# The order of VectorE's instructions and the gates on GpSimd's gathers in a software pipeline of graph attention

## The chip, the cores and the metric

The kernel runs on one core of a Trainium2 chip. The metric is the device time of one execution in microseconds (us).

## The reference

A graph of 6250 nodes with 64 features and 206,250 edges, sorted by their destination. One layer of mean aggregation is followed by three layers of attention (heads: 2, 2, 1; 64 channels in all). Cut to what matters, with H heads of C channels:

```python
def _transformer_conv(x, src, dst, eattr, ...):
    q, k, v = x @ Wq + bq, x @ Wk + bk, x @ Wv + bv     # each reshaped to (n, H, C)
    e = (eattr @ We).reshape(-1, H, C)
    kj = k[src] + e
    alpha = jnp.sum(q[dst] * kj, axis=-1) / jnp.sqrt(jnp.float32(C))
    m = jax.ops.segment_max(alpha, dst, num_segments=n)
    a = jnp.exp(alpha - m[dst])
    s = jax.ops.segment_sum(a, dst, num_segments=n)
    a = a / (s[dst] + 1e-16)
    vj = v[src] + e
    out = jax.ops.segment_sum(a[..., None] * vj, dst, num_segments=n)
    return out.reshape(n, H * C) + x @ Ws + bs
```

## The kernel before

The edges are cut into blocks of 1024, 8 columns (T) of 128 edges. Each pass over the edges has 202 steps, one for each block: one pass for the mean layer, three for attention. Between the passes are node phases that work out the tables of k, v and q for the nodes.

An attention pass is a software pipeline of five stages, Z, A, B, C, D, each a step later than the one before it. In step t the engines work on stage Z of block t+2, A of t+1, B of t, C of t-1 and D of t-2. What each engine does in a step, and in which order, is written out by hand: `vector_step` (L990), `tensor_step` (L1070), `scalar_step` (L1133), and the lists `order` (L666) from which the semaphore values are worked out. Every instruction of such a list raises its engine's progress semaphore by one, and `after(e, engine, op, s)` waits until an instruction of block s is done. `hold(e)` is an increment of a spare semaphore behind such a wait.

VectorE's 24 instructions of a step, by the names used below:
- Stage A: `kj` (L752) and `vj` (L757) add the edge term to the gathered rows of k and v; `prod` (L763) multiplies by q, `alpha` (L768) sums over the channels; `flag` (L774) and `scan` (L782) make the running maximum over edges with one destination; `O` (L720) is the one-hot matrix of edge and destination.
- Stage Z: `OT` (L731) is the transposed one-hot, from int16 to bf16, 1024 elements in each partition; `cont` (L743) and `last` (L737) mark the borders of segments.
- Stage B: `fhi`, `fm` (L785), `flo`, `cr`, `X`, `Mhi`, `Mm`, `Mlo`, `df` spread the maxima over the edges.
- Stage C: `d1`, `d`, and `vals` (L837), which multiplies vj by the weights.
- Stage D: `facc` (L863) and `acc` (L873) rescale and add up the result in `acc`.

GpSimd does one thing in an attention pass: for each block eight indirect DMAs, one for each column j (L1355, `gathers`), each of which fetches 128 rows of the table KV by the indices in `sdn` into the buffer `G`. There are three buffers G, so gathers may run ahead of VectorE. The first blocks are unrolled, where only gather 0 waits, for `vj` of three blocks ago. In the loop the table `gates` says which gather waits for what: gather 0 of block s for `aT` (a TensorE transpose, in the step after which `alpha` is known) of block s-3. `kj` of block s waits until all eight gathers of block s have landed.

TensorE's aggregation `agg` of block dt writes pG, which `facc` and `acc` read; before it stands a wait for `acc` of block dt-1. SyncE loads the indices, edge features and q rows of a block, behind a wait for `O` of three blocks ago (L1247).

Of the kernel before, what the change touches and what calls it, by code (L numbers as in the profile page):

```python
# [66 lines left out]
def build(nc, z, a, ctx):  # L67
    B, NCOL, NT, SM = z.blocks, z.nc, z.tiles, z.smax
# [15 lines left out]
    acc = sb("acc", [66, NCOL])  # L84
# [570 lines left out]
    def edge_pass(name, kind, l, heads, qtab, kvtab, eat):  # L655
# [8 lines left out]
        AR = 64 + H  # L664
        if att:
            order = {  # L666
                "V": ["A kj", "A vj", "B fhi", "B fm", "B flo", "B cr", "Z OT", "A prod", "A alpha", "C d1", "C d",
                      "Z cont", "Z last", "A flag", "A O", "B X", "B Mhi", "B Mm", "B Mlo", "B df", "C vals",
                      "D facc", "D acc", "A scan"],
                "P": ["B Fb", "A q", "D agg7", "B Mn", "Z e", "A aT", "B Me"],  # L670
                "A": ["A tb", "A lb", "A Ob", "C w", "B fb", "B fbw"],
            }
        else:
            order = {
                "V": ["C acc", "Z O", "Z OT"],
                "P": ["A e", "B agg7", "A q"],
                "A": ["A relu"],
            }
# [20 lines left out]
        def after(e, k, o, s):  # L699
            e.wait_ge(prog[k], val(k, o, s))  # L700
# [24 lines left out]
        def v_OT(e, s):  # L725
            u = s.slot
            if att:
                ge16(e, s_l, NL, s)
            else:
                ge16(e, s_d, 1, s)  # L730
            return e.tensor_scalar(OTs[u][:, :, :].rearrange("p j m -> p (j m)"), db[u][:, :],  # L731
                                   bfp[:, bass.ds(s.value(), 1)], None, ALU.is_equal)
# [257 lines left out]
        def vector_step(e, t, on):  # L990
            pV = prog["V"]
            zt, at, bt, ct, dt = t + 2, t + 1, t, t - 1, t - 2
            if not att:
                if "C" in on:
                    v_acc(e, ct).then_inc(pV, 1)
                else:
                    missing(e, "V", t, "acc", "acc")
                if "Z" in on:
                    v_O(e, zt).then_inc(pV, 1)
                    v_OT(e, zt).then_inc(pV, 1)  # L1000
                else:
                    missing(e, "V", t, "O", "OT")
                return
            if "A" in on:
                v_kj(e, at).then_inc(pV, 1)
                v_vj(e, at).then_inc(pV, 1)
            else:
                missing(e, "V", t, "kj", "vj")
            if "B" in on:
                v_fhi(e, bt).then_inc(pV, 1)  # L1010
                v_fm(e, bt).then_inc(pV, 1)
                v_flo(e, bt).then_inc(pV, 1)
                v_cr(e, bt).then_inc(pV, 1)
            else:
                missing(e, "V", t, "fhi", "cr")
            if "Z" in on:
                v_OT(e, zt).then_inc(pV, 1)
            else:
                missing(e, "V", t, "OT", "OT")
            if "A" in on:  # L1020
                v_prod(e, at).then_inc(pV, 1)
                v_alpha(e, at).then_inc(pV, 1)
            else:
                missing(e, "V", t, "prod", "alpha")
            if "C" in on:
                if "B" not in on:
                    after(e, "P", "Me", ct)
                v_d1(e, ct).then_inc(pV, 1)
                v_d(e, ct).then_inc(pV, 1)
            else:  # L1030
                missing(e, "V", t, "d1", "d")
            if "Z" in on:
                v_cont(e, zt).then_inc(pV, 1)
                v_last(e, zt).then_inc(pV, 1)
            else:
                missing(e, "V", t, "cont", "last")
            if "A" in on:
                v_flag(e, at).then_inc(pV, 1)
                v_O(e, at).then_inc(pV, 1)
            else:  # L1040
                missing(e, "V", t, "flag", "O")
            if "B" in on:
                v_X(e, bt).then_inc(pV, 1)
                v_Mhi(e, bt).then_inc(pV, 1)
                v_Mm(e, bt).then_inc(pV, 1)
                v_Mlo(e, bt).then_inc(pV, 1)
                if "A" not in on:
                    after(e, "A", "fbw", bt - 1)
                v_df(e, bt).then_inc(pV, 1)
            else:  # L1050
                missing(e, "V", t, "X", "df")
            if "C" in on:
                v_vals(e, ct).then_inc(pV, 1)
            else:
                missing(e, "V", t, "vals", "vals")
            if "D" in on:
                if "A" not in on:
                    after(e, "P", "agg7", dt)
                if "C" not in on:
                    after(e, "V", "acc", dt - 1)  # L1060
                v_facc(e, dt).then_inc(pV, 1)
                v_acc(e, dt).then_inc(pV, 1)
            else:
                missing(e, "V", t, "facc", "acc")
            if "A" in on:
                v_scan(e, at).then_inc(pV, 1)
            else:
                missing(e, "V", t, "scan", "scan")

        def tensor_step(e, t, on):  # L1070
            pP = prog["P"]
            zt, at, bt, dt = t + 2, t + 1, t, t - 2
            if not att:
                if "A" in on:
                    p_e0(e, at).then_inc(pP, 1)
                else:
                    missing(e, "P", t, "e", "e")
                if "B" in on:
                    for j in range(T - 1):
                        p_agg(e, bt, j)  # L1080
                    p_agg(e, bt, T - 1).then_inc(pP, 1)
                else:
                    missing(e, "P", t, "agg7", "agg7")
                if "A" in on:
                    for j in range(T - 1):
                        p_q(e, at, j)
                    p_q(e, at, T - 1).then_inc(pP, 1)
                else:
                    missing(e, "P", t, "q", "q")
                return  # L1090
            if "B" in on:
                p_Fb(e, bt).then_inc(pP, 1)
            else:
                missing(e, "P", t, "Fb", "Fb")
            if "A" in on:
                for j in range(T - 1):
                    p_q(e, at, j)
                p_q(e, at, T - 1).then_inc(pP, 1)
            else:
                missing(e, "P", t, "q", "q")  # L1100
            if "D" in on:
                after(e, "V", "acc", dt - 1)
                hold(e)
                p_fac(e, dt)
                for j in range(T - 1):
                    p_agg(e, dt, j)
                p_agg(e, dt, T - 1).then_inc(pP, 1)
            else:
                missing(e, "P", t, "agg7", "agg7")
            if "B" in on:  # L1110
                p_Mc(e, bt)
                for j in range(T):
                    p_Mn(e, bt, j)
                p_Mn(e, bt, T).then_inc(pP, 1)
            else:
                missing(e, "P", t, "Mn", "Mn")
            if "Z" in on:
                p_e0(e, zt)
                p_e1(e, zt).then_inc(pP, 1)
            else:  # L1120
                missing(e, "P", t, "e", "e")
            if "A" in on:
                p_aT(e, at).then_inc(pP, 1)
            else:
                missing(e, "P", t, "aT", "aT")
            if "B" in on:
                for j in range(T - 1):
                    p_Me(e, bt, j)
                p_Me(e, bt, T - 1).then_inc(pP, 1)
            else:  # L1130
                missing(e, "P", t, "Me", "Me")
# [203 lines left out]
                for c in range(3 + z.peel, 6 + z.peel):  # L1335
                    pool_step(e, At(i, c))

        gates = {0: ("P", "aT", 3)}

        AHEAD = 2  # L1340

        def gathers(e, s):
            u = s.slot
            ge16(e, s_i, 1, s)
            hold(e)
            for j in range(T):
                if isinstance(s.i, int):
                    if j == 0 and not fresh(s):
                        after(e, "V", "vj", s - 3)
                        hold(e)  # L1350
                elif j in gates:
                    engine, op, behind = gates[j]
                    after(e, engine, op, s - behind)
                    hold(e)
                e.indirect_dma_start(G[u][:, j, :], None, kvtab,  # L1355
                                     bass.IndirectOffsetOnAxis(ap=sdn[u][:, j:j + 1], axis=0)).then_inc(s_g[u], 16)
# [155 lines left out]
```

## Time and profile before

| what | value |
|---|---|
| runs, median (lowest to highest) | 6918.2 us (6917.99 to 6919.75), 3 runs |
| the profiled execution | 6918.2 us, its span 6916.5 us |
| TensorE busy | 4425.5 us (64%) |
| VectorE busy | 4457.8 us (64%) |
| ScalarE busy | 969.0 us (14%) |
| GpSimd busy | 4794.7 us (69%) |
| mean DMA rate | 98 GB/s |

Busy time counts only the execution of instructions, not the time an engine takes between two of them or waits. The three attention passes are alike and much the longest part.

### The profile page before, as it was taken

Reading aid. Unit: us, or ns where it says so; the run is one execution under the profiler, and the core shown is the slowest. Engines: PE = TensorE matmul, PEld = TensorE weight load, DVE = VectorE, ACT = ScalarE, POOL = GpSimd, SP = SyncE. Lnnn points to the kernel's source line nnn. Section 1 sums busy time; section 2 is a strip of 40 time slices with the busy share of each in tenths; the row PEclk is TensorE's granted clock in tenths of the full one; section 3 lists DMA queues with packets and bytes.
Section 4 is the critical chain, followed back from the end, with each engine's and each line's share of the span. In section 5 each row is a group of like instructions: output and inputs, shape, how many; then the busy total and the mean of one; then the engine's idle time right before and its main releaser. Section 6 shows DMA issues by size and latency. Waiting matters only on the chain. (4 is left out here: it accounts for less than half of the span.)

```text
span 6916.5 us, 148957 instructions
## 1 busy us (share of the span) xinstructions
PE 4425.5 (64%) x36620; PEld 3474.0 (50%) x36620; DVE 4457.8 (64%) x15728; ACT 969.0 (14%) x4122; POOL 4794.7 (69%) x5118
## 2 busy tenths in 40 slices
PE   6996666666666666666666666666656666666665
PEld 5775444444444446444444444446444444444444
DVE  6556666666666666666666666666666666666666
ACT  2222111111111112111111111112111111111110
POOL 2224777777777774777777777775777777777775
PEclk8996555555555555555555555555555555555555
DMA  4553333333333333333333333333333333333333
GB/s 120 159 159 96 94 94 95 94 96 95 94 94 93 95 94 90 95 94 96 95 95 95 93 94 94 94 93 88 99 93 96 94 94 95 94 97 95 94 94 75
DMA packets 687686, 675.83 MB, mean 98 GB/s; under 512 B 369234, under 2 KB 506388, under 8 KB 687636
## 3 DMA queue, kind: packets, MB, share of 16 engines
q0 software_dynamic: 161600, 320.52, 19.4%
q1 hardware_dynamic: 496944, 301.76, 16.5%
q10 hardware_dynamic: 29092, 52.97, 2.6%
q8 instruction: 20, 0.33, 0.0%
q14 instruction: 30, 0.25, 0.0%
HBM read 652.96 MB, written 21.67 MB: 98 GB/s over the span
## 5 line engine op out<-in xcount | busy, mean ns | idle before, releaser
L1355 POOL DMA_INDIRECT Gall<-KV,sdn x4848 | 4647.3, 959 | 1516.8 <-issue 1337.4
L752 DVE TENSOR_TENSOR kj<-Gall,pE 128x512 f32<-128x512 f32 x606 | 416.7, 688 | 1896.3 <-DMA Gall<-KV,sdn 1894.2
L946 PE MATMUL pG<-O,vals 128*66 128x42 f32 (+1 forms) x10784 | 1297.9, 308 | 0.7 <-ACTq L988 0.7
L946 PEld LDWEIGHTS pG<-O,vals 128*66 128x66 f32 (+1 forms) x10784 | 1207.1, 223 | 46.9 <-ACT vals L982 26.1
L932 PE MATMUL pY<-fw,Ob 128*42 128x6 bf16 (+1 forms) x4848 | 257.9, 176 | 1056.8 <-DVE cr L805 1043.7
L959 ACT ACTIVATE fw<-lm 128x16 bf16<-128x16 f32 (+1 forms) x606 | 135.9, 224 | 5348.4 <-DVE O L720 5348.4
L932 PEld LDWEIGHTS pY<-fw,Ob 128*42 128x42 bf16 x4848 | 223.0, 121 | 1111.3 <-issue 1111.0
L879 PE MATMUL pE<-bd,ea 128*128 128x256 f32 x1212 | 739.9, 714 | 13.5 <-PEq L988 13.5
L939 PEld LDWEIGHTS pM<-Mb,OTs 42*128 42x128 bf16 x4848 | 178.1, 101 | 952.7 <-issue 952.7
L884 PE MATMUL pE<-bd,ea 128*128 128x256 f32 x1212 | 642.7, 634 | 0.0
L916 PE MATMUL pS<-ident,Fs 16*128 16x16 f32 (+1 forms) x606 | 152.2, 251 | 733.3 <-DVE Fs L782 729.5
L939 PE MATMUL pM<-Mb,OTs 42*128 42x6 bf16 (+1 forms) x4848 | 212.3, 163 | 545.5 <-DVE df L823 543.4
L916 PEld LDWEIGHTS pS<-ident,Fs 16*128 16x128 f32 (+1 forms) x606 | 107.6, 177 | 768.1 <-issue 768.1
L837 DVE TENSOR_TENSOR vals<-vj,vals 128x512 f32<-128x512 f32 x606 | 420.0, 693 | 69.4 <-ACT vals L977 6.8
L884 PEld LDWEIGHTS pE<-bd,ea 128*128 128x128 f32 x1212 | 407.9, 337 | 108.5
L720 DVE SCALAR_TENSOR_TENSOR O<-sdn,bf,iof 128x336 f32<-128x336 int32 x808 | 451.6, 559 | 5.6 <-DVEq L988 1.3
L731 DVE TENSOR_SCALAR OTs<-db,bfp 128x1024 bf16<-128x1024 int16 x808 | 418.1, 517 | 21.3 <-DMA dr<-in_dr 18.2
L768 DVE TENSOR_REDUCE al<-kj 128x16 f32<-128x512 f32 (+1 forms) x606 | 416.4, 687 | 20.9
L757 DVE TENSOR_TENSOR vj<-Gall,pE 128x512 f32<-128x512 f32 x606 | 412.0, 680 | 0.0
L763 DVE TENSOR_TENSOR kj<-kj,pQ 128x512 f32<-128x512 f32 x606 | 409.5, 676 | 1.3 <-PEq L988 0.7
L1252 POOL DMA_DIRECT2D sdn<-in_sdn x202 | 108.8, 539 | 400.1 <-DVE OTs L731 333.8
L904 PE MATMUL pQ<-qw,OTs 128*128 128x64 bf16 x4848 | 367.7, 241 | 8.6 <-DVEq L988 6.1
(185 smaller groups left out, 6275.8 us busy)
## 6 DMA issues: line engine op xcount, KB each, us to landing
db<-D SPq DMA_DIRECT2D x606, 256.0 KB
ea<-in_ea SPq DMA_DIRECT2D x606, 128.0 KB
Gall<-KV,sdn POOLq DMA_INDIRECT x4848
db<-D ACTq DMA_DIRECT2D x202, 256.0 KB, 3.7
qw<-QT SPq DMA_DIRECT2D x1818, 5.2 KB
dr<-in_dr SPq DMA_DIRECT2D x1212, 4.0 KB
ea<-in_ea SPq DMA_DIRECT2D x202, 64.0 KB, 3.7
sdn<-in_sdn SPq DMA_DIRECT2D x606, 12.0 KB
```

Source lines behind the costliest of these rows:

```text
L720: return e.scalar_tensor_tensor(O[u][:, :, :], sdn[u][:, T:2 * T].unsqueeze(2).to_broadcast([128, T, W]), bf[:, bass.ds(s.value(), 1)], io ...
L731: return e.tensor_scalar(OTs[u][:, :, :].rearrange("p j m -> p (j m)"), db[u][:, :], bfp[:, bass.ds(s.value(), 1)], None, ALU.is_equal)
L752: return e.tensor_tensor(kj[:, :, :], G[u][:, :, 0:64], pE[u][:, :].rearrange("p (j c) -> p j c", c=64), ALU.add)
L757: return e.tensor_tensor(vj[u][:, :, :], G[u][:, :, 64:128], pE[u][:, :].rearrange("p (j c) -> p j c", c=64), ALU.add)
L763: return e.tensor_tensor(kj[:, :, :], kj[:, :, :], pQ[:, :].rearrange("p (j c) -> p j c", c=64), ALU.mult)
L768: return e.tensor_reduce(al[u][:, 0:H * T].rearrange("p (h j) -> p j h", h=H), kj[:, :, :].rearrange("p j (h c) -> p j h c", h=H), AX.X, A ...
L837: return e.tensor_tensor(vals[u][:, :, 0:64].rearrange("p j (h c) -> p j h c", h=H), vj[u][:, :, :].rearrange("p j (h c) -> p j h c", h=H) ...
L879: return e.matmul(pE[u][:, 0:256], ea[u][:, 0:128], bd32[:, l, :], start=True, stop=True)
L884: return e.matmul(pE[u][:, 256:512], ea[u][:, 128:256], bd32[:, l, :], start=True, stop=True)
L932: return e.matmul(pmn[:, j, :], lhs, rhs, start=False, stop=j == T)
L946: return e.matmul(sums[u][0:AR, 0:W], vals[u][:, j, 0:AR], O[u][:, j, :], start=j == 0, stop=j == T - 1)
L1355: e.indirect_dma_start(G[u][:, j, :], None, kvtab, bass.IndirectOffsetOnAxis(ap=sdn[u][:, j:j + 1], axis=0)).then_inc(s_g[u], 16)
```

## The change

`OT` moves in VectorE's order from behind `cr` to behind `df`; `facc` and `acc` move from behind `vals` to behind `O`; `scan` now stands ahead of `vals`, which comes last. The wait in front of `agg` asks for `vals` of the same block instead of `acc` of the block before. The table of gates gives six of the eight gathers a wait on VectorE, gather 0 for `Mlo` of block s-3 instead of TensorE's `aT`, and the gathers 1, 2, 5, 6 and 7, which had none, for `scan`, `vals`, `vj`, `prod` and `flag`. All values of the semaphore follow from the lists. The mean pass is not touched.

```diff
             order = {
-                "V": ["A kj", "A vj", "B fhi", "B fm", "B flo", "B cr", "Z OT", "A prod", "A alpha", "C d1", "C d",
-                      "Z cont", "Z last", "A flag", "A O", "B X", "B Mhi", "B Mm", "B Mlo", "B df", "C vals",
-                      "D facc", "D acc", "A scan"],
+                "V": ["A kj", "A vj", "B fhi", "B fm", "B flo", "B cr", "A prod", "A alpha", "C d1", "C d", "Z cont",
+                      "Z last", "A flag", "A O", "D facc", "D acc", "B X", "B Mhi", "B Mm", "B Mlo", "B df", "Z OT",
+                      "A scan", "C vals"],
...
             if "D" in on:
-                after(e, "V", "acc", dt - 1)
+                after(e, "V", "vals", dt)
                 hold(e)
                 p_fac(e, dt)
...
-        gates = {0: ("P", "aT", 3)}
+        gates = {0: ("Mlo", 3), 1: ("scan", 2), 2: ("vals", 4), 5: ("vj", 1), 6: ("prod", 1), 7: ("flag", 1)}
...
                 elif j in gates:
-                    engine, op, behind = gates[j]
-                    after(e, engine, op, s - behind)
+                    op, behind = gates[j]
+                    after(e, "V", op, s - behind)
                     hold(e)
```

In `vector_step` the calls of v_OT, v_facc with v_acc, and v_scan move in the same way.

## Rows read from the trace of the kernel before

**Rows 1.** Stretches of the first and the last attention pass: GpSimd's gathers, clock, DMA share.

```profile
601.00:2651.00 2050.00, 1555.96 (x1616) 0.50 0.38 95
...
4827.00:6867.00 2040.00, 1542.71 (x1616) 0.50 0.38 95
sum 6137.00, POOL 4647.31; mean POOL 1549.10
```

**Rows 2.** Groups by line; then the gathers' durations (min/median/max) and landing.

```profile
L1355 POOL DMA_INDIRECT Gall<-KV,sdn x4848 | 4647.3, 959 | 1516.8 <-issue 1337.4
L752 DVE TENSOR_TENSOR kj<-Gall,pE 128x512 f32<-128x512 f32 x606 | 416.7, 688 | 1896.3 <-DMA Gall<-KV,sdn 1894.2
...
L1355 POOL DMA_INDIRECT Gall<-KV,sdn x4848: 940/944/1537, 601.0 to 6865.0; - x194
...
DMA to landing us min/median/max: 2.5/3.9/5.4
```

**Rows 3.** Waits of SyncE's DMA queue: us in total, times, longest.

```profile
SPq L708 <- DVE O L720: 2969.6, 596, 6.5
```

**Rows 4.** Order in time, VectorE, one step: start us, us, instruction.

```profile
2002.30 0.69 DVE L752 TENSOR_TENSOR kj<-Gall,pE 128x512 f32<-128x512 f32 x1 [3.08 <-DMA Gall<-KV,sdn]
...
2004.01 0.59 DVE L731 TENSOR_SCALAR OTs<-db,bfp 128x1024 bf16<-128x1024 int16 x1
...
2006.35 0.28 DVE L774 TENSOR_TENSOR flg<-tb 16x127 f32<-16x127 f32 x1
2006.56 0.55 DVE L720 SCALAR_TENSOR_TENSOR O<-sdn,bf,iof 128x336 f32<-128x336 int32 x1
...
2007.62 0.15 DVE L823 TENSOR_TENSOR df<-X,Mm 42x2 f32<-42x2 f32 x1
...
2007.87 0.69 DVE L837 TENSOR_TENSOR vals<-vj,vals 128x512 f32<-128x512 f32 x1
...
2008.58 0.21 DVE L863 TENSOR_SCALAR acc<-acc,pG  x1
...
2008.94 0.40 DVE L782 TENSOR_TENSOR_SCAN Fs<-flg,pS 16x128 f32<-16x128 f32 x1
...
2012.21 0.69 DVE L752 TENSOR_TENSOR kj<-Gall,pE 128x512 f32<-128x512 f32 x1 [2.87 <-DMA Gall<-KV,sdn]
```

**Rows 5.** GpSimd in the same step: gathers 5 and 7 and the next gather 0.

```profile
2005.90 0.94 POOL L1355 DMA_INDIRECT Gall<-KV,sdn  x1 [0.31 <-issue]
...
2008.39 0.99 POOL L1355 DMA_INDIRECT Gall<-KV,sdn  x1 [0.30 <-issue]
2009.69 0.94 POOL L1355 DMA_INDIRECT Gall<-KV,sdn  x1 [0.30 <-issue]
```

**Rows 6.** Three long gathers and what VectorE had under way.

```profile
882.02 0.48 DVE L731 TENSOR_SCALAR OTs<-db,bfp 128x1024 bf16<-128x1024 int16 x1
882.42 0.68 DVE L763 TENSOR_TENSOR kj<-kj,pQ 128x512 f32<-128x512 f32 x1
...
882.19 1.13 POOL L1355 DMA_INDIRECT Gall<-KV,sdn  x1 [0.30 <-issue]
...
1027.48 0.27 DVE L774 TENSOR_TENSOR flg<-tb 16x127 f32<-16x127 f32 x1
1027.68 0.55 DVE L720 SCALAR_TENSOR_TENSOR O<-sdn,bf,iof 128x336 f32<-128x336 int32 x1
...
1027.62 1.43 POOL L1355 DMA_INDIRECT Gall<-KV,sdn  x1 [0.30 <-issue]
...
2088.71 0.69 DVE L837 TENSOR_TENSOR vals<-vj,vals 128x512 f32<-128x512 f32 x1
...
2089.08 1.14 POOL L1355 DMA_INDIRECT Gall<-KV,sdn  x1 [0.30 <-issue]
```

**Rows 7.** The first and the last of the 4848 gathers.

```profile
601.05 1.01 POOL L1355 DMA_INDIRECT Gall<-KV,sdn  x1 [12.70 <-DMA KV<-stg]
...
6865.05 0.94 POOL L1355 DMA_INDIRECT Gall<-KV,sdn  x1 [0.30 <-issue]
```

More of the change, by code:

```diff
@@ L1015, in vector_step @@
                 missing(e, "V", t, "fhi", "cr")
[L1016 to L1019, printed above, removed]
             if "A" in on:
@@ L1041, in vector_step @@
                 missing(e, "V", t, "flag", "O")
+            if "D" in on:
+                if "A" not in on:
+                    after(e, "P", "agg7", dt)
+                if "C" not in on:
+                    after(e, "V", "acc", dt - 1)
+                v_facc(e, dt).then_inc(pV, 1)
+                v_acc(e, dt).then_inc(pV, 1)
+            else:
+                missing(e, "V", t, "facc", "acc")
             if "B" in on:
@@ L1051, in vector_step @@
                 missing(e, "V", t, "X", "df")
+            if "Z" in on:
+                v_OT(e, zt).then_inc(pV, 1)
+            else:
+                missing(e, "V", t, "OT", "OT")
+            if "A" in on:
+                v_scan(e, at).then_inc(pV, 1)
+            else:
+                missing(e, "V", t, "scan", "scan")
             if "C" in on:
@@ L1055, in vector_step @@
                 missing(e, "V", t, "vals", "vals")
[L1056 to L1059, printed above, removed]
-                    after(e, "V", "acc", dt - 1)
[L1061 to L1068, printed above, removed]
         def tensor_step(e, t, on):
@@ L1101, in tensor_step @@
             if "D" in on:
-                after(e, "V", "acc", dt - 1)
+                after(e, "V", "vals", dt)
                 hold(e)
```

## The prediction

> **What bounds the kernel now.** I read the stretches first, then the groups by line, the waits, and then the order in time of one step. The page's list of engines is no help by itself: no engine is over 70% busy. The stretches show that the three attention passes fill most of the span [rows 1]: 2050 us the first, 2040 the last, 6137 in sum for 606 steps, or 10.1 us a step; each holds 1616 gathers that keep GpSimd busy some 1550 us. The rest, 6916.5 - 6137 = 780 us of setup, mean pass and node phases, is left as it is by the change.
>
> The groups show why a share of 69% hides the bound [rows 2]. The 4848 gathers are busy for 4647.3 us, 959 ns each, and stand behind 1516.8 us of idle time, 1337.4 of it put down to "issue": GpSimd waits for nobody, it needs 0.30 us between two gathers. A gather is 940 ns at the least and 944 at the median, and up to 1537. So the pace of a step is 8 x (0.944 + 0.300) = 9.95 us of bare gathers, plus (959 - 942) ns x 4848 = about 80 us over the kernel by which some gathers are longer. VectorE instead waits 1894.2 us in front of `kj` for the gathered rows, 3.1 us a step. Anything that shortens or rearranges VectorE's work changes nothing directly; only what lengthens a gather or the gap between gathers moves the time.
>
> **What lengthens a gather.** The order in time answers this [rows 6]. The gather at 1027.62 took 1.43 us; `O` began at 1027.68 while `flag` was under way since 1027.48, and ended at 1028.23. Take the time from 0.12 us after the gather's start to `O`'s end: 1028.23 - 0.12 - 1027.62 = 0.49, and the gather lost 1.43 - 0.94 = 0.49. The gather at 2089.08 took 1.14, with `vals` from 2088.71 to 2089.40: 2089.40 - 0.12 - 2089.08 = 0.20, and that is what it lost. The gather at 882.19 took 1.13, with `OT` from 882.02 to 882.50: 0.19 by the same sum, 0.19 lost. So a gather that is 0.12 us old while `flag`, `O`, `vals` or `OT`, begun before it, still runs, is held until that ends. One that was there first loses nothing: at 2005.90 it takes 0.94 although `O` starts at 2006.56 [rows 4, 5]. By that rule I put the long gathers of the whole trace (counted over all 4848, the first and the last are in [rows 7]) to their causes: `vals` 35 us, `flag` with `O` 26, `OT` 7, `fhi` and `fm` 7, the small rest is spread out. That makes up the 80.
>
> The Trainium skill (SBUF — State Buffer, Who interferes with whom) says that a VectorE instruction with two SBUF inputs contends with a GpSimd one that reads SBUF, one in a two-port mode with any, and that whoever issues first holds the shared ports. The trace agrees with the order of issue. The same section infers that `tensor_tensor` does not stall descriptor generation; by that only `OT` could cost anything here, but `vals` is a tensor_tensor and the 1.14 us gather under it says otherwise.
>
> **The change, part by part.**
> 1. *Five more gates* (gathers 1, 2, 5, 6, 7; gather 0 changes its own). Do they block? kj of the step of rows 4 starts at 2002.30. Gather 7 starts at 2008.39, 6.1 us after it, gather 0 of the next block at 2009.69, 7.4 us after, and the data of gather 7 let the next kj go at 2012.21 [rows 4, 5]. Each gate asks for an instruction of the VectorE step that is under way: gather 7 for `flag`, which ended 4.3 us after kj and will end at about 3.9; gather 0 for `Mlo`, which ends at about 5.2; `scan` and `vals` end at about 6.1 and 6.8, and gathers 1 and 2 come at 8.6 and 9.9. So each has 2 to 3 us in hand. The landing (2.5 to 5.4 us, median 3.9) seldom is late by more than that. Blocking: 0 to 5 us, I take 0.
>  Do they cost by being there? Gather 0 in the loop has two waits and two marker increments in front of it, others have none, and the idle time before it is 0.30 like that before the rest: the row at 2009.69 is a gather 0 [rows 5]. The work in between lies under the 0.94 us of the gather before. Cost 0. If that cover were not there, the nearest row for a price is the gap itself: half of it again, 0.15 us for each of five, would be 0.75 x 606 = 450 us; this bound I hold to be far off.
> 2. *OT leaves the place after cr*. In [rows 6] `prod` starts 0.40 after `OT`, and as a rule 0.42. So `prod`, `alpha`, `flag` and `O` all come 0.42 us sooner after kj: `flag` to 3.6, `O` to 3.8, ending at 4.35 (now 4.0, 4.2, 4.8 as a rule; this step was 0.06 late).
>  Gather 5 starts 3.6 us after kj here (2005.90), and over the 606 steps between 3.4 and 4.1 in eight of ten. Today it is mostly there before `O`. From the new place it is held when it starts between 3.67 (flag is under way) and 4.35 - 0.12 = 4.22. Of 601 gathers that start 3.2 to 4.45 us after a kj, 388 lie in that stretch and are short of its end by 119 us in sum; with only those after `O`'s own start it is 225 and 47 us. The same two counts for the old place give 37 and 5.5 us, and the long gathers there came to 26, which is two thirds of the way up. The same two thirds of 47 to 119 is 93 us. Net +67 us, bounds +21 and +93.
> 3. *facc and acc go before X*. `facc` starts at 2008.58 and `scan` at 2008.94, so the pair takes 0.36 us. Neither causes long gathers. `vals` used to wait for ScalarE: df starts at 2007.62, lasts 0.15, and vals starts at 2007.87. The read of the accumulator's address, which lay under a `vals` of 0.69, now has an `O` of 0.55 as cover; 0 to 0.15 us later from there on. GpSimd doesn't see that but by phase.
> 4. *OT after df, scan, then vals last*. df will start at 3.8 + 0.48 + 0.36 + 0.58 = 5.2, `OT` at 5.3 to 5.8, `scan` at 5.7, `vals` at 6.05 to 6.75. Gather 7 stands at 5.84 to 6.61 in eight of ten. Held by the new vals are starts between 6.13 and 6.63: 355 of 600, 99 us in sum, against 35 now. (For the old place the count gives 34 us, so it can be trusted.) But part 2 has shifted those behind a held gather 5: they go on at 4.22 + 1.24 = 5.46, where the new `OT` is under way and can hold gather 6 by 5.8 - 0.12 - 5.46 = 0.22 us, or miss it by a hair; a gather 7 after both comes at 6.7 to 6.95, past the end of vals' stretch. The two exclude each other for much of the steps. I take 60 us for vals and 30 for OT, less the 35 and 7 of now: +48 us. Bounds: 0 to +120.
> 5. *What else moves.* `agg` now waits for `vals` instead of `acc` of the step before: that ends at 6.8 and PE has until `acc`, 4 us after the next kj. `scan` ends earlier than before, so the transposes behind it are early. SyncE's loads wait for `O` (2969.6 us in all, [rows 3]), which comes 0.42 us sooner: no loss. VectorE's step has the same instructions, about 7 us, and still waits 3 us for the gather. All 0.
>
> The profiled execution was 6918.2 us, as the median, for a span of 6916.5. Sum: 6918 + 67 + 48 = 7033; I give 7030. About 0.2%, 14 us, is what a measurement here can tell from no change.
>
> **Rivals.**
> - *The new places miss the gathers.* What counts is where `flag`, `O`, `OT` and `vals` start relative to gathers 5, 6 and 7. If the new VectorE order has the step 0.3 us tighter or looser than my timetable, or the phases lock in a kinder way after the first hold, the long gathers vanish. Were all gone: 6918 - 80 = 6838; more likely half, 6880. It decides when the four instructions hold no more than today: with vals and OT at their lower bound, when fewer than about 110 gathers 5 are held (26 us at 93 / 388 = 0.24 each). Against it: the count over real starts in part 2 does not depend on anything after `O`. 0.17.
> - *Nothing measurable.* The gains and losses cancel, or `flag` and `O` hold a gather less than they did: 6918. By the skill's inference above, as a mechanism here, only OT is left, 7 us now and 10 to 40 later: 6920 to 6950; the row of the 1.14 us gather speaks against it. 0.13 in all within 0.2%.
> - *The gates cost in the gap.* Five waits and increments not hidden; at 0.05 us each 0.25 x 606 = 150 us on top of the sum: 7180, or alone 7070. The equal gap of gather 0 is against it. 0.07.
> - *The gates bind.* Then GpSimd would be led by VectorE: needs landings over 6 us, and the longest is 5.4. 0.01.
>
> **How the numbers follow.** Longer gathers as summed: 0.62, own range 6960 to 7100 (terms at +21 and +20, to +93 and +90). Slower altogether 0.62 + 0.07 + 0.01 = 0.70, same 0.13, faster 0.17. The range from 6900 to 7110 leaves out most of the faster case and of the gap's cost.
>
> **What would show it.** VectorE's order in time: OT after df, `O` ending 4.3 us after kj. The gather's mean up from 959 to 983 ns (115 us over 4848), the longest ones at position 5 under `O`, then 7 under `vals`, or 6 under `OT`. Idle before the gathers unchanged at about 1517 us with 0.30 each; any more is the gates'. kj's wait goes up by 0.2 us a step. Wrong if the mean is at or under 959, or if the gaps before gated gathers are over 0.30.

## The result and the profile after

The changed kernel takes 7155.15 us (median of 4, 7152.58 to 7170.39) against 6918.26 us: ratio 1.0344, 95% interval 1.0327 to 1.0361. It is slower by 237 us, as forecast in sign, and more than twice as much as forecast (+112), outside the range. Its profiled execution took 7176.55 us, 258.35 more than that of before (6918.2).

The groups hold the answer to [rows 2]. First two groups by line of the changed kernel (busy us, mean ns, idle before), then, from the view of the tile, the durations of the gathers (min/median/max in ns):

```profile
L1355 POOL DMA_INDIRECT Gall<-KV,sdn x4848 | 4905.9, 1012 | 1515.8 <-issue 950.6
L752 DVE TENSOR_TENSOR kj<-Gall,pE 128x512 f32<-128x512 f32 x606 | 417.0, 688 | 2225.1 <-DMA Gall<-KV,sdn 2222.5
```

```profile
L1355 POOL DMA_INDIRECT Gall<-KV,sdn x4848: 940/944/1767, 600.9 to 7122.8; - x194
```

The gathers are busy for 4905.9 - 4647.3 = 258.6 us more, and that is the whole difference of the two profiled executions. The idle time before them is 1515.8 against 1516.8: six gates instead of one cost nothing here. The median gather is 944 ns as before, so a part of them has become much longer.

One step in order of time shows which. It answers to [rows 4, 5] (start us, us, instruction). First VectorE; then GpSimd with gather 7 of one block, gathers 5, 6 and 7 of the next:

```profile
2005.13 0.69 DVE L752 TENSOR_TENSOR kj<-Gall,pE 128x512 f32<-128x512 f32 x1 [4.16 <-DMA Gall<-KV,sdn]
...
2008.92 0.55 DVE L720 SCALAR_TENSOR_TENSOR O<-sdn,bf,iof 128x336 f32<-128x336 int32 x1
...
2010.48 0.62 DVE L731 TENSOR_SCALAR OTs<-db,bfp 128x1024 bf16<-128x1024 int16 x1
2011.03 0.40 DVE L782 TENSOR_TENSOR_SCAN Fs<-flg,pS 16x128 f32<-16x128 f32 x1
2011.35 0.66 DVE L837 TENSOR_TENSOR vals<-vj,vals 128x512 f32<-128x512 f32 x1
```

```profile
2002.42 0.94 POOL L1355 DMA_INDIRECT Gall<-KV,sdn  x1 [0.30 <-issue]
...
2009.91 0.94 POOL L1355 DMA_INDIRECT Gall<-KV,sdn  x1 [0.30 <-DVE acc L873]
2011.16 1.67 POOL L1355 DMA_INDIRECT Gall<-KV,sdn  x1 [0.30 <-DVE OTs L731]
2013.13 0.94 POOL L1355 DMA_INDIRECT Gall<-KV,sdn  x1 [0.30 <-issue]
```

VectorE stands within 0.2 us of where the prediction put it (medians: flag 3.6, O 3.8, OT 5.35, scan 5.9, vals 6.2 us after kj; forecast for the last three 5.3, 5.7, 6.05). Two things were not foreseen.

First, gather 6 at 2011.16 took 1.67 us. By the rule of the prediction it should have been safe: 0.12 us after its start, at 2011.28, `scan` was running, under which no gather had been held before, and `vals` began only at 2011.35. Yet it was held to the end of vals: 2012.01 - 0.12 - 2011.16 = 0.73, and it lost 1.67 - 0.94 = 0.73. Over all steps, 343 gathers begin under scan and 328 are held; the 15 others began within 0.05 us of scan's start. In the kernel before it was 72 and none; but there the instruction behind scan is the next `kj`, which still waits for its data.

Second, the gathers stand elsewhere. Gather 7 here is that at 2002.42; its data let kj go at 2005.13, 1.77 us after its end. This time from the end of gather 7 to the start of kj is called the landing from here on. In [rows 4, 5] it was 2012.21 - 2009.38 = 2.83. The medians over 606 steps are 1.76 and 2.73. Since GpSimd goes on at its own pace and kj comes sooner after gather 7, all gathers stand later after kj: gathers 5, 6, 7 at 4.8, 6.05 and 7.9 us instead of 3.9, 5.1 and 6.4. So gather 5 goes free behind `O`, and gather 6 begins just under `scan`.

Sorted by the instruction at whose end the held gather goes on, the long gathers sum to 339 us (80 before): vals 281 (33), O 22 (20), OT 14 (6), flag 3 (3); the rest, 18 (19), ends with none of the four. These sums, here and below, are the busy time of all 4848 gathers of a trace less 0.942 us for each.

### The profile page after: what moved, and what is told of

Same layout as the page of the kernel before. It is cut to its first block and busy times, and to the rows that moved or that the text cites. A ratio compares the mean times of both kernels' runs of the same rounds, so it can differ in the third digit from the quotient of the medians.

```text
span 7174.9 us, 154717 instructions
## 1 busy us (share of the span) xinstructions
PE 4422.2 (62%) x36620; PEld 3475.0 (48%) x36620; DVE 4453.4 (62%) x15728; ACT 997.8 (14%) x4122; POOL 5053.5 (70%) x5118
## 5 line engine op out<-in xcount | busy, mean ns | idle before, releaser
L1355 POOL DMA_INDIRECT Gall<-KV,sdn x4848 | 4905.9, 1012 | 1515.8 <-issue 950.6
L884 PEld LDWEIGHTS pE<-bd,ea 128*128 128x128 f32 x1212 | 407.5, 336 | 109.2
L837 DVE TENSOR_TENSOR vals<-vj,vals 128x512 f32<-128x512 f32 x606 | 396.8, 655 | 3.0 <-DVEq L988 1.8
L879 PEld LDWEIGHTS pE<-bd,ea 128*128 128x128 f32 x1212 | 303.5, 311 | 24.7 <-issue 14.6
```

What stands on the lines that cost most here:

```text
L837: return e.tensor_tensor(vals[u][:, :, 0:64].rearrange("p j (h c) -> p j h c", h=H), vj[u][:, :, :].rearrange("p j (h c) -> p j h c", h=H) ...
L879: return e.matmul(pE[u][:, 0:256], ea[u][:, 0:128], bd32[:, l, :], start=True, stop=True)
L884: return e.matmul(pE[u][:, 256:512], ea[u][:, 128:256], bd32[:, l, :], start=True, stop=True)
L1355: e.indirect_dma_start(G[u][:, j, :], None, kvtab, bass.IndirectOffsetOnAxis(ap=sdn[u][:, j:j + 1], axis=0)).then_inc(s_g[u], 16)
```

## The experiments

The runs were made on several chips, each with the kernel before beside it; ratios are to that. The kernel before itself took 6918 us (median) with the result above, 6970 beside the first four experiments, 6939 beside the next four and 6960 beside the test of the loads. On three more chips, called slow below, it took some 8700 us; they are told of last. Each chip had one set of runs, so chip and time can't be told apart. So a ratio near 1 says little here without the trace. Its profiled execution at 6918.2 us is the yardstick for the rows: in every trace of the fast chips the time is that plus what the gathers' busy and idle time are above 4647.3 + 1516.8, within 4 us.

**Gates alone.**

```diff
-        gates = {0: ("P", "aT", 3)}
+        gates = {0: ("Mlo", 3), 1: ("scan", 2), 2: ("vals", 4), 5: ("vj", 1), 6: ("prod", 1), 7: ("flag", 1)}
...
```

> The old order of VectorE with the six new gates. If the gates are free (the gaps of the changed kernel sum to 1515.8 us as before): 6918 us within 15, mean of a gather 959 ns, idle before gathers 1517 us. If the gates are part of the loss, because they tie the gathers to VectorE: at least 60 us slower and the idle before gathers grows.

7031.98 us, ratio 1.0084 (1.0061 to 1.0107): 62 us above the kernel before on this chip, with more idle time, so the second expectation by its numbers. Group of the gathers, and a gather 1:

```profile
L1355 POOL DMA_INDIRECT Gall<-KV,sdn x4848 | 4714.3, 972 | 1561.6 <-issue 1064.3 <-DVE cr L805 78.0 <-DVE flg L774 54.0
```

```profile
3431.56 0.94 POOL L1355 DMA_INDIRECT Gall<-KV,sdn  x1 [1.62 <-issue]
```

The idle time grew by 45 us, made of 45 gaps of 0.66 to 2.02 us in front of gather 1, one every 13 steps of a pass, with no wait for anybody. Some of the same steps show such a gap in other kernels: 2 in the changed kernel, 32 of 0.5 to 1.5 us in the changed kernel with three waits (below), none in the order alone, and 45 of some 2.0 us in a kernel with the one old gate on a slow chip (below). Why they come is open. The larger part of what the trace has above that of the kernel before is the long gathers, 147 us instead of 80 (vals 60, O 38, OT 23), for the gathers stand elsewhere: gather 6 at 5.8 and gather 7 at 7.25 us after kj, with a landing of 2.36. So VectorE is not waited for in the old order either, which was the mechanism of that expectation, but the gates were not free there.

**Order alone.** The changed kernel with the old table of gates.

> The new order of VectorE with the one old gate. If the order alone makes the loss through longer gathers: 7155 us within 20, mean of a gather 1012 ns, most of it at gather 6. If order and gates only cost together: under 7050.

7174.23 us, ratio 1.0291 (1.0271 to 1.0310), long gathers 339 us, gather 6 held in 495 of 606 steps. The ratio is smaller than that of the changed kernel because the kernel before took 6970 us on this chip.

```profile
L1355 POOL DMA_INDIRECT Gall<-KV,sdn x4848 | 4905.8, 1012 | 1513.5 <-issue 1469.4 <-DMA KV<-stg 28.4 <-DVE fm L785 4.5
```

Busy time and mean are those of the changed kernel (4905.9, 1012): the order alone makes the loss, and with this order the gates have no part in it.

**vals waits for scan.** The changed kernel with one more wait.

```diff
             after(e, "A", "w", s)
+            after(e, "V", "scan", s + 2)
             return e.tensor_tensor(
```

> The changed kernel with one more wait: vals starts only when scan is done. Theory A: an instruction that needs the shared ports holds them from when it is queued behind a running one, so that vals behind scan holds for 1.05 us instead of 0.65; with the wait it can't queue, and a gather that begins under scan is not held. The sum by which gathers are longer falls from 337 us to under 220, time under 7050. Theory B: scan itself or any work in that place holds the gather: time stays at 7155 within 20, gathers are still held when they begin under scan. The wait itself costs VectorE under 0.1 us a step, of the 3.7 us that it idles.

6910.66 us, ratio 0.9912 (0.9894 to 0.9929). One wait took away the whole loss: 264 us against the order alone on the same chip. Long gathers 74 us, 6 less than in the trace of the kernel before. That the ratio is 0.9% under 1 isn't explained by that; it compares with 6970 us on this chip, where the kernel before was not profiled.

```profile
L1356 POOL DMA_INDIRECT Gall<-KV,sdn x4848 | 4640.4, 957 | 1514.8 <-issue 776.8
```

The same situation as above, in order of time:

```profile
5468.19 0.40 DVE L782 TENSOR_TENSOR_SCAN Fs<-flg,pS 8x128 f32<-8x128 f32 x1
5468.62 0.69 DVE L838 TENSOR_TENSOR vals<-vj,vals 128x512 f32<-128x512 f32 x1
```

```profile
5468.31 0.95 POOL L1356 DMA_INDIRECT Gall<-KV,sdn  x1 [0.31 <-issue]
```

The gather begins under scan and takes 0.95; 279 begin so, none is held, though vals starts within 0.5 us behind them, as in the changed kernel. scan itself holds nobody, theory B falls. What holds is vals when it stands behind a running scan with nothing left to wait for. In the kernel before it stood behind df, and there is idle time in front of it, as far as the trace names it for ScalarE. The groups of vals, before and changed:

```profile
L837 DVE TENSOR_TENSOR vals<-vj,vals 128x512 f32<-128x512 f32 x606 | 420.0, 693 | 69.4 <-ACT vals L977 6.8
L837 DVE TENSOR_TENSOR vals<-vj,vals 128x512 f32<-128x512 f32 x606 | 396.8, 655 | 3.0 <-DVEq L988 1.8
```

Theory A, that it takes the ports while still queued, explains it; the trace shows only that the wait ends it. The wait also changed the places (landing 2.04, gathers 5, 6, 7 at 4.5, 5.8, 7.1), so not all of the 259 us is the queueing itself.

**O waits for flag,** in the kernel before.

```diff
                 after(e, "P", "agg7", s - 3)
+                after(e, "V", "flag", s)
```

> The kernel before with one more wait: O starts only when flag is done. Theory A: gathers are no longer held through O from a start under flag; the 26 us by which flag and O lengthen gathers fall by 5 to 15, time 6900 to 6915. Theory B: no change from the wait but a later O: 6918 within 8 or slower by some us as O comes nearer to the next gather.

6911.91 us, ratio 0.9911 (0.9896 to 0.9927). O holds for 12.5 us in sum against 20, and wherever it holds a gather it had begun at least 0.16 us before the gather did (in the kernel before it held gathers that began up to 0.16 us ahead of it, while it was queued behind flag). That is as theory A has it. The kernel gains nothing by it: the long gathers sum to 82 us (80 in the kernel before), as vals has 37 instead of 33, and the profiled execution took 6918.07 us, as that of the kernel before did. The time is in the forecast range, but the ratio is again one to the 6970 us of this chip.

**The kernel before again.**

> The kernel before, unchanged, for its trace on the same chip as the runs beside it. Where it ran at 6970 us the gathers should be longer by the 52 us against 6918 (some 130 us in sum over 0.942 each instead of 80), not the gaps. If the gaps grew, the theory that only long gathers move this kernel is wrong.

6934.43 us, ratio 0.9993 (0.9983 to 1.0003), the same. This was not the chip of the four runs above, so the 130 us expected at 6970 stay untested. On this one the profiled execution took 6926.69 us, 8.5 more than the yardstick, with long gathers of 90 us (9 more) and an idle time of 1517.7 (1 more): the difference between these two traces is in the long gathers, not the gaps.

**Three waits,** vals for scan, O for flag, OT for df, on the changed kernel, and the like (OT for cr, O for flag, vals for df) on the kernel before.

> The changed kernel with waits that keep OT, O and vals from being queued behind df, flag and scan. Theory A (held from the queue): also the 9 us of O and some of OT's 26 go; 6880 to 6905 us, sum of long gathers 50 to 70 us. Theory B (only vals behind scan matters): as with that wait alone, 6911 within 8.

> The kernel before with waits that keep OT, O and vals from being queued behind cr, flag and df. vals already waited for ScalarE, so by theory A its wait does nothing; OT behind cr of 0.2 us: a few us. 6900 to 6912 us, about that of the kernel before with the wait of O alone. If more than 15 us below that one, the queue holds in more places than the runs have shown.

Ratios 1.0075 (1.0062 to 1.0088) and 1.0171 (1.0157 to 1.0184): both expectations missed, and with them the idea that more waits are better. In the changed kernel the long gathers sum to 137 us, 80 of them by vals, which holds gather 7. The kernel before with three waits, one step (VectorE, then gather 7):

```profile
4003.08 0.69 DVE L754 TENSOR_TENSOR kj<-Gall,pE 128x512 f32<-128x512 f32 x1 [3.15 <-DMA Gall<-KV,sdn]
...
4009.03 0.69 DVE L840 TENSOR_TENSOR vals<-vj,vals 128x512 f32<-128x512 f32 x1 [0.20 <-ACT vals L980]
```

```profile
4009.30 1.24 POOL L1358 DMA_INDIRECT Gall<-KV,sdn  x1 [0.30 <-issue]
```

The waits put OT 0.25, O 0.43 and vals 0.52 us later after kj. vals now begins at 6.05, gather 7 at 6.35, and it is held in some 540 of 606 steps (in the rows: 4009.72 - 0.12 - 4009.30 = 0.30, lost 0.30); O holds gather 6 in some 350. Long gathers 221 us: vals 149, O 48, OT 9. Each of flag, O, OT and vals, where it holds a gather, had begun at least 0.1 us before it: queueing is gone, the place alone does this.

**vals last,** in the kernel before: facc, acc and scan ahead of vals, OT, flag and O as they were. As in the change, `agg` then waits for `vals` of its block.

```diff
-  ... "B df", "C vals", "D facc", "D acc", "A scan"],
+  ... "B df", "D facc", "D acc", "A scan", "C vals"],
...
-                after(e, "V", "acc", dt - 1)
+                after(e, "V", "vals", dt)
```

> The kernel before with one part of the change: facc, acc and scan go ahead of vals, so that vals stands behind scan, ready to go; OT, flag and O stay. Theory A: vals holds from under scan, gathers that begin there are held for up to 1.05 - 0.12 us and the time rises by 50 to 250 us. Theory B (the loss is OT's or O's new place): within 20 us of the kernel before.

7037.11 us, ratio 1.0145 (1.0128 to 1.0162); long gathers 192 us, vals 95 of them, O 56, OT 25. 85 gathers begin under scan and 69 are held. vals behind scan is enough for a loss; for the large one more gathers must stand there.

**Where the landing comes from.** Over the traces of the fast chips it falls as gather 7 stands later than `O`, behind which SyncE's loads of a block wait (medians, us). Gates alone falls out of the line by some 0.3:

| kernel | gather 7 after O's start | landing after its end |
|---|---|---|
| before, three waits | 1.7 | 2.79 |
| before | 2.2 | 2.73 |
| before, vals last | 2.5 | 2.40 |
| changed, three waits | 3.0 | 2.09 |
| before, gates alone | 3.1 | 2.36 |
| changed, vals waits for scan | 3.3 | 2.04 |
| changed | 4.1 | 1.76 |

The largest load of a block is that of `db`, 256 KB. SyncE issues it here at these times, in the kernel before (the step of rows 4) and in the changed one:

```profile
2008.41 0.33 SPq L1266 DMA_DIRECT2D db<-D  x1
...
2010.76 0.33 SPq L1266 DMA_DIRECT2D db<-D  x1
```

Gather 7 ended at 2009.38 in the kernel before, 1.0 us after that, and in the changed one at 2013.13 + 0.94 = 2014.07, 3.3 us after. Sorted by this time and not by kernel, the steps of ten traces of the fast chips (all but the test below) fall together, gates alone too; a kernel with over 50 steps in a class lies within 0.25 us of the value given:

| end of gather 7 after the start of the large load, us | 1.0 | 1.5 | 2.0 | 2.5 | 3.0 | 3.5 |
|---|---|---|---|---|---|---|
| landing, median us | 2.8 | 2.6 | 2.25 | 2.0 | 1.7 | 1.7 |
| steps | 1672 | 849 | 1394 | 988 | 597 | 370 |

The test moves the loads and not the order, in the changed kernel:

```diff
-                after(e, "V", "O", s - 3)
+                after(e, "V", "scan", s - 3)
```

> The changed kernel with SyncE's loads of a block waiting for scan instead of O, 1.9 us later. Theory L (the loads stand in the way of a gather's data): gather 7, 7.9 us after kj, is again near the loads, its data take 2.3 to 2.8 us instead of 1.76, all gathers start 0.6 to 1.0 us sooner after kj, gather 6 leaves its place under scan and vals and O holds gather 5 more often, as the prediction had it; the time changes by more than 30 us, either way. Rival (the landing has to do with where gather 7 stands, not with the loads): landing 1.8 within 0.2, gather 6 at 6.05, 7155 to 7175 us. On a chip with late loads, where the kernel before takes 8700 us, the run says nothing of this.

7101.37 us, ratio 1.0205 (1.0188 to 1.0222). The landing is 2.53 in the median (1.76 without), and mostly up to 3.6; gathers 5, 6, 7 start 4.0, 5.5, 6.9 us after kj, 0.6 to 1.1 sooner. Long gathers 244 us: O 59, OT 49, vals 119. With the loads behind O, gather 7 at 7.0 and 7.1 us after kj had a landing of 2.09 and 2.04 (three waits, vals waits for scan), so the rival, that its place sets the landing, falls: the loads do slow the gathers' data. Within this trace, the 182 steps whose gather 7 ended some 0.5 us after the start of the large load have a landing of 3.37, the 149 where that load began 1 us after the end have 1.72. The change had taken the loads out of the way of gather 7: `O` came 0.4 us sooner, and the shorter landing and the held gathers then put gather 7 itself 1.5 us later after kj. Of 138 gathers that begin under scan, 124 are held.

**The chips on which the kernel before takes 8700 us.** The expectations speak of one chip with late loads; it was three, and no trace shows that the loads are what makes them slow. Four kernels, two with SyncE's loads moved (waiting for X of block s-4 in the changed kernel, for scan of block s-3 in the kernel before) and two with OT behind X, vals waiting for scan, and six gates or one. They ran twice, and one of them a third time, on a third such chip; the kernel before took 8690 to 8720 us beside them.

> The changed kernel; SyncE's loads of a block wait for X instead of O, so they start some 0.5 us later in the step, as late after kj as before the change. Theory L: a gather's landing is slowed by these loads; the change brought them forward, so the last gather's data came 1.76 us after its end instead of 2.73, which moved all gathers from 3.9, 5.1, 6.4 us after kj to 4.8, 6.05, 7.9, with gather 6 just under scan and vals. With the loads later the landing goes back to 2.3 us or more, gather 6 is off that place and the time falls under 7100. Rival: the landing is shorter because gather 7 itself stands later; then it stays at 1.8 within 0.2 and the time at 7155 to 7175.

> The kernel before; SyncE's loads wait for scan instead of O, some 2.2 us later in the step. Theory L: the landing of the last gather (median 2.6 to 2.7 us after its end) changes by more than 0.4 us, because the loads fall otherwise on it, and with it the places of the gathers and the sum of long gathers (80 to 90 us before). Rival: the landing does not depend on the loads, and landing and time stay (within 0.1 us and 15 us).

> The changed kernel with the wait of vals for scan (6911 us before), and OT moved on from behind df to behind X, 0.5 us earlier, to 4.8 to 5.3 us after kj, between gathers 5 and 6. If place alone decides, OT's 26 us of long gathers go and the sum falls from 78 to 45 to 60 us: 6880 to 6900 us, 0.985 to 0.990 of the kernel before. If OT behind another instruction holds as vals did behind scan, no gain or a loss.

> The same with the one old gate. If the gates only wait for what is long done: the same time within 10 us. If the five more cost (the old order with new gates showed 47 us more idle time before gathers): faster by up to 40 us.

> The changed kernel with SyncE's loads waiting for X instead of O, again, where the kernel before runs at 6918 to 6970 us. Theory L (the loads slow the landing of a gather): landing of the last gather back from 1.76 to 2.3 us or more after its end, gather 6 no longer at 6.05 us after kj, time under 7100. Rival (the landing is set by where gather 7 stands): 1.8 within 0.2, time 7155 to 7175.

> The kernel before with SyncE's loads waiting for scan instead of O, 2.2 us later. Theory L: landing differs from 2.6 to 2.7 us by more than 0.4, gathers shift against kj by as much, and the sum of long gathers leaves 80 to 90 us. Rival: landing within 0.1, time within 15 us.

> The changed kernel with vals waiting for scan and OT behind X, 4.8 to 5.3 us after kj. Place alone: sum of long gathers 45 to 60 us, 0.985 to 0.990 of the kernel before. If OT behind another instruction holds as vals behind scan did: no gain over 0.991.

> The same with the one old gate. If gates cost nothing where they do not block: within 10 us of the one with six gates. If five more cost: faster by up to 40 us.

> The changed kernel with vals waiting for scan and OT behind X, at 4.8 to 5.3 us after kj, between the places of gathers 5 (4.5) and 6 (5.8) that the wait alone showed. By place alone OT's 26 us of long gathers go, the sum falls from 78 to 45 to 60 us, and the ratio to the kernel before from 0.991 to 0.985 to 0.990. If the gathers' places shift with it (they hang on the landing, which moved by up to 1 us between the kernels), the sum can come out anywhere from 50 to 150 and the ratio up to 1.005. On a chip with late loads it says nothing.

Ratios: changed with later loads 1.0014 and 1.0010; before with later loads 1.1143 and 1.1135; OT behind X 1.0269, 1.0265 and 1.0291; with the old gate 1.0502 and 1.0508. None of them can answer what was asked, since another thing sets the pace. The waits of the first (us in total, times, longest):

```profile
DVE X L809 <- remote: 1793.7, 459, 7.5
...
POOL Gall L1355 <- DVE OTs L731: 791.3, 264, 14.4
...
DVE kj L752 <- DMA Gall<-KV,sdn: 377.0, 124, 6.6
```

VectorE hardly waits for gathers there (377 us against 2222 in the changed kernel above), but for something that the trace calls remote, that is, no instruction in it. And where VectorE is late GpSimd waits for it too: 791 us behind OT. In the kernel with OT behind X the gates wait 1794 us for scan:

```profile
POOL Gall L1359 <- DVE Fs L782: 1794.2, 527, 16.7
```

In the kernel before with later loads GpSimd waits 2580.6 us for the load of the indices, `sdn`. The kernel before itself was not profiled on these chips. Here six gates are faster than one (1.027 against 1.050), the opposite of a cost. Why these chips are slow, and whether OT behind X would win on the others, stays open.

## Why the prediction was wrong

- *GpSimd sets the pace, and only longer gathers or gaps move the time:* right, to 0.3 us (258.6 for 258.35).
- *Gates (part 1):* right for the changed kernel: no blocking, idle 1516 us. Order alone gives the same busy time. The argument, that the work of a gate is hidden, doesn't hold in general: with the old order the same gates came with 45 us of gaps.
- *OT leaves the place after cr (part 2):* the times of flag and O were right to 0.05 us. The term was +67; measured +3 (O and flag, 25 us against 22), because gather 5 was no longer there. With the loads moved back, and the landing near what the prediction took for fixed, it came to 59, two thirds of the 93.
- *scan ahead of vals (part 4) is the step that failed.* It sized vals at 60 us and OT at 30; they measured 281 and 14. Two assumptions in it were false. That a gather is held only by an instruction that has begun: vals, ready behind scan, holds from under it. The prediction had noted this for O behind flag and did not carry it over to vals, which by being put last no longer had anything to wait for. And that the places of the gathers after kj stay as they were but for the holds: they hang on the landing, and the landing on `O`, for SyncE's loads wait for it. The step of part 5 was the hole: "SyncE's loads wait for `O` [...], which comes 0.42 us sooner: no loss."
- *The sum:* the forecast had the sign, with +115 us of long gathers for the +259 measured. Its parts were off both ways, by 64 us too much in part 2 and by 208 too little in part 4 (vals and OT +256 for +48), so the sum is nearer than its larger part by luck. Its own range took part 4 at +20 to +90, whose bounds it had given as 0 to +120; the wider ones would not have reached either.
- How much is whose: with the wait for scan the whole loss goes (74 us of long gathers), with the loads moved back 244 of 339 us remain. That speaks for the queueing as the larger cause; their shares can't be parted, as each hold moves the places again.
- *The rival "The new places miss the gathers"* came true for O alone; the other three did not happen in the changed kernel.
- The Trainium skill (SBUF — State Buffer, Who interferes with whom) infers that `tensor_tensor` does not stall descriptor generation. The 281 us by which vals, a `tensor_tensor`, holds gathers are against it. Its rule that whoever issues first gets the shared pair for the whole instruction agrees with the gathers held under vals, if issue includes the queue.

## What to carry to other kernels

Where one engine makes descriptors for small gathers back to back and another works beside it, draw up both timetables and look at the moment just after each gather's start: what matters is which instruction is under way there, or ready behind the one under way. Moving work that the path doesn't contain can cost percents, through holds and through the transfers that it releases. A wait in front of the holding instruction may remove a hold, but it moves all that follows, so each such edit must be measured, and on more than one chip.

## What was not expected of the hardware

- A VectorE instruction with two SBUF inputs that is ready behind a running one held a gather as if it had begun: 328 of 343 gathers, up to 0.8 us each; with a semaphore wait in front, 0 of 279.
- The landing of a gather's last rows fell from 2.8 to 1.7 us with the time since another queue's 256 KB load (1.0 to 3.0 us).
- One unchanged kernel took 6918, 6939, 6960 and 6970 us in four sets of runs, the last three on different chips, and 8693 to 8719 us on three more chips, each used in one set.
- GpSimd had gaps of 0.66 to 2.02 us every 13th step in one kernel; in near copies the same steps had them in part or not at all.
